# Order of the q, k and v weight loads between layers of a six-layer attention network

## What is computed

```python
def attn_layer(x, Wqkv, qs, ksc, Wo):
    qkv = x @ Wqkv                               # 128 x 3072 weights: q, k, v of 16 heads of 64
    q, k, v = jnp.split(qkv, 3, -1)
    ...
    q = l2norm(q) * qs
    k = l2norm(k) * ksc
    ...                                          # rotary tables on q and k
    out = local_attention(q, k, v)               # windows of 32 tokens, each sees itself and the one before
    return out @ Wo
for i in range(DEPTH):
    x = attn_layer(shift_tokens(x), Wqkv[i], ...) + x
    x = ffn_layer(shift_tokens(x), ln_g[i], ...) + x
```

## Time and profile before

| | |
|---|---|
| median of 3 runs | 2058.47 us (2055.76 to 2065.01) |
| the profiled execution, its own time | 2059.67 us |
| its span, first to last instruction | 2057.6 us |
| PE busy | 1890.4 us, 92% of the span |
| DVE, ACT, POOL busy | 66%, 58%, 58% |
| the network, first k projection of tile 0 to that of tile 95 | about 142 to 1799 us |
| mean granted clock of TensorE | 0.958 of full speed |

### The profile page before, as it was taken

How to read it: one execution, slowest core, us unless ns; L and a number is a source line. 1 busy time by engine, 2 the same in 40 slices (tenths; PEclk the granted TensorE clock), 3 DMA queues, 4 the chain that set the end, 5 groups by cost and what they waited for, 6 DMA issues and landing times. The chain is left out here.

```text
span 2057.6 us, 71282 instructions
## 1 busy us (share of the span) xinstructions
PE 1890.4 (92%) x30632; PEld 1191.6 (58%) x30632; DVE 1348.7 (66%) x1564; ACT 1188.7 (58%) x2030; POOL 1201.5 (58%) x1291
## 2 busy tenths in 40 slices
PE   5867999899999899998999998999989999986898
PEld 5734666565666466665656664666656566653444
DVE  5646777677777577776677775777766777742533
ACT  4425666466766666664667656666746676553333
POOL 0118777667776677776677766777766777630000
PEclk9979999999999999999999999999999999997888
DMA  1023222222222322223222222222232222201000
GB/s 46 0 86 74 69 63 64 82 62 73 72 61 64 79 70 73 62 64 82 64 72 72 62 63 78 71 72 61 66 83 62 73 72 62 64 20 46 6 5 11
DMA packets 84770, 125.11 MB, mean 61 GB/s; under 512 B 26208, under 2 KB 31976, under 8 KB 84336
## 3 DMA queue, kind: packets, MB, share of 16 engines
q1 hardware_dynamic: 84464, 120.64, 23.2%
HBM read 21.98 MB, written 1.05 MB: 11 GB/s over the span
## 5 line engine op out<-in xcount | busy, mean ns | idle before, releaser
L318 POOL TENSOR_TENSOR qkn<-t 128x1024 f32<-128x1024 f32 x192 | 452.5, 2357 | 258.7 <-DVE t L715 251.5
L309 POOL TENSOR_TENSOR qkn<-qkn,rn 128x512 f32<-128x512 f32 x384 | 392.5, 1052 | 14.6 <-POOL rn L303 1.3
L711 DVE TENSOR_TENSOR t<-qk_ps,rot 128x1024 f32<-128x1024 f32 x192 | 229.1, 1193 | 110.7 <-ACT sq L585 109.6
L326 POOL TENSOR_TENSOR pn<-pexp,rden 128x512 f32<-128x512 f32 x192 | 196.2, 1043 | 171.6 <-DVE rden L699 171.6
L585 ACT ACTIVATE sq<-qk_ps 128x1024 f32<-128x1024 f32 x192 | 196.7, 1025 | 147.9 <-PE qk_ps L383 125.2
L447 PEld LDWEIGHTS sc_ps<-prT,v_win 64*64 64x64 f32 x12288 | 199.8, 136 | 126.0 <-issue 125.8
L725 DVE TENSOR_REDUCE sums<-sq 128x16 f32<-128x1024 f32 x192 | 233.1, 1214 | 43.2 <-ACT sq L585 37.5
L578 ACT COPY prT<-ring 128x512 f32<-128x512 f32 x192 | 112.2, 584 | 243.2 <-PE ring L431 243.2
L398 PE MATMUL ring<-ident,qkn 128*128 128x128 f32 x1536 | 228.0, 282 | 23.2 <-POOL qkn L309 18.7
L715 DVE TENSOR_TENSOR t<-qk_ps,rot 128x1024 f32<-128x1024 f32 x192 | 232.9, 1213 | 0.0
L447 PE MATMUL sc_ps<-prT,v_win 64*64 64x32 f32 x12288 | 221.2, 221 | 7.8 <-DVE pr L687 6.4
(11 more groups left out here) (238 smaller groups left out, 2836.6 us busy)
## 6 DMA issues: line engine op xcount, KB each, us to landing
v_win<-v_tok SPq DMA_DIRECT2D x1488, 64.0 KB, 2.0
wqkv<-in_w_qkv SPq DMA_DIRECT2D x18, 512.0 KB, 4.1
wo<-in_w_o SPq DMA_DIRECT2D x6, 512.0 KB, 3.9
w<-in_w SPq DMA_DIRECT2D x6, 341.0 KB, 3.3
w<-in_w SPq DMA_DIRECT2D x6, 192.0 KB, 3.0
r_xtok<-in_x SPq DMA_DIRECT2D x4, 256.0 KB, 3.5
amask<-in_att_mask SPq DMA_DIRECT2D x1, 1024.0 KB
out_x<-xo SPq DMA_DIRECT2D x4, 256.0 KB, 2.3
```

The source lines that it names most:

```text
L309: nc.gpsimd.tensor_tensor(by_head(quarter(qkn, f)), by_head(quarter(qkn, f)), rn[:, 8 * f:8 * (f + 1)].unsqueeze(2).to_broadcast([P, 8, DH ...
L318: nc.gpsimd.tensor_tensor(half(qkn, k), half(t1, k), half(t2, k), ALU.add).then_inc((q_added, k_added)[k], 1)
L711: nc.vector.tensor_tensor(by_head(half(t1, k)), by_head(of), rot[:, l % 2, 2 * k, s:s + 1, :].to_broadcast([P, HEADS, DH]), ALU.mult).then ...
```

## The change

For the last tile of a layer SP now waits for k_full and loads k, waits for v_full and loads v, then does the waits and the 14 v moves as before, and after them waits for q_full and loads q. The loads of layer 0 are as they were, and nothing is changed on the other engines.

```diff
                     r, t = g // TILES, g % TILES
                     l, b = r // B, r % B
-                    if t == TILES - 1 and b == B - 1 and l + 1 < DEPTH:
-
-                        sp.wait_ge(q_full, 2 * (g + 1))
-                        load_qkv(l + 1, 0, s_wq)
+                    last_of_layer = t == TILES - 1 and b == B - 1 and l + 1 < DEPTH
+                    if last_of_layer:
+
                         sp.wait_ge(k_full, 2 * (g + 1))
                         load_qkv(l + 1, 1, s_wk)
+                        sp.wait_ge(v_full, 2 * (g + 1))
+                        load_qkv(l + 1, 2, s_wv)
                     sp.wait_ge(v_copied, 2 * (g + 1))
                     if g > 2:
 
                         sp.wait_ge(av_full, g - 2)
...
-                    if t == TILES - 1 and b == B - 1 and l + 1 < DEPTH:
-                        load_qkv(l + 1, 2, s_wv)
+                    if last_of_layer:
+                        sp.wait_ge(q_full, 2 * (g + 1))
+                        load_qkv(l + 1, 0, s_wq)
                     if l > 0 and b == 0 and t == TILES - 1:
```

## The result

The changed kernel takes 2005.3 us (median of 4 runs, 2001.07 to 2007.18) against 2059.75 us before (median of 4, 2055.76 to 2065.01): ratio 0.9731, 95% interval 0.9704 to 0.9759. Two further sets of five runs gave medians of 2002.9 and 2001.6, against 2058.0 and 2057.9 before. The profiled execution of the changed kernel, one of the four, took 2007.18 us with a span of 2005.3 us; that this span equals the median is chance.

A forecast was written before the change was run, and what follows sets the result against it. PE, busy 92%, sets the pace and idles for weights at changes of layer. Terms 11.7 + 31.8 + 9.5 - 2.5 give 50.5 us; the yardstick's 52.2 was taken, giving 2006.3 us against the median, range 2000 to 2018.

The forecast's parts named there:

- the sum: Whole kernel: the forecast's reckoning, 50.5 us by its terms and 52.2 us by the yardstick, of which 52.2 was taken.
- Steps 1 and 2: Changes of layer: k load issued first, v load next; PE's waits for k (11.7 us) and v (31.8 us) go.
- The yardstick: Five stage pairs at changes of layer, 218.6 us together, should take 33.28 us each as inside a layer: 52.2 us gained.
- Step 3: v matmuls at each change of layer: without a pause ahead they take the fast time, 1.9 us less each, 9.5 us.
- rival A: v matmuls at changes of layer stay slow because of freshly landed weights, not the pause: 9.5 us kept, 2015.8 us; chance 0.05.
- Step 4: v moves of a layer's last tile no longer wait for q_full: they start 4 us earlier and cost nothing.
- Step 5: q load after the moves: issued at 399.1, lands at 402.9, due at 405.8, 2.9 us to spare; the tightest place.
- rival B: q load at changes of layer lands 1.6 us late, 8 us in five: 2014.3 us; chance 0.08.
- Step 6: Transposes after each change of layer wait for POOL again, 0.5 us each: 2.5 us come back.
- Rival C: POOL becomes the bound behind the changes of layer: 20.5 us come back, 2026.8 us; chance 0.03.
- The terms: Listed effects at changes of layer: k wait 11.7, v wait 31.8, slow matmuls 9.5, less POOL 2.5: 50.5 us.
- Rival E: Slower: q held back on SP; gain of 10.4 us per change used up at landing 416.2; 2069 if 12.6 late; chance 0.02.

## Why the prediction was right

The forecast was 2006.3 us and the measured time 2005.3. The mechanism is the forecast's; that the two times meet within 1 us is in part luck. The gain by the medians of the three sets was 54.5, 55.1 and 56.3 us, 2 to 4 us above the 52.2 of the sum. The 95% intervals of the ratios include 52.2, and no run shows where more would come from. Point by point:

- **Steps 1 and 2** (the waits of k and v go) held: both rows are gone. That it was the weights that ended both waits is shown by the runs in which one of the two loads comes early and the other not, with v's wait rising to 43.3 us when k alone is early, and k's staying at 11.9 us when v alone is early. Their two terms are not independent, which the prediction did not say: k's 11.7 us are worth nothing unless v comes early too. The yardstick, which measures both together, does not depend on this.
- **Step 3** (the slow v matmuls go) held, and its reason too: with a pause alone, in front of weights that had landed long before, the group takes 3.75 us at a granted clock of 0.50. The prediction's point against rival A, that a k group behind a landing and a pause of 2.08 us stays fast, was weaker than it looked: with v alone early, k groups behind waits of 1.98 and 2.24 us were slow. It is the run with the pause alone that decides.
- **Step 4** (the v moves start 4 us earlier and cost nothing) held. The run that puts q ahead of them, and starts them 4 us later again, takes the same time.
- **Step 5** (q 2.9 us before its due time) held at the first change: q was issued 17.1 us after the last tile's k projection began, against 17.0 by the sum, and landed in 3.8 us. It was never waited for, but at the fourth change the issue came 1.4 us later than computed and the landing took 5.1 us, which left 0.3 us. So rival B came nearer than its chance of 0.08 suggests, and that no wait appeared there owes something to luck. Rival B had taken the price of lateness as 1 us for each us; the runs with q held back show that slow matmuls come on top, 0.3 to 3.2 us at a change.
- **Step 6** (2.5 us of waits for POOL come back) held. In the five pairs the transposes did not wait for POOL before, and now wait 0.51 to 0.58 us in each, 2.8 us in all. The wait over the network is a poorer measure: it was 21.2, 20.3 and 19.5 us in three profiles of the changed kernel, so that 21.2 less 18.7 is just the 2.5 forecast is chance. Rival C did not appear.
- **The sum.** The yardstick, the same pair of stages inside a layer, gave 52.2 us; the pairs became 51.9 us shorter. The terms gave 50.5, and the 1.4 us between lie in small gaps and slow matmuls that were not listed, such as the k group of 2.52 us at the second change, shown below.
- **Rival E** was far off in time, but its price was too low: with the 2.5 us of slow matmuls that a wait brought in the mean in the first run with q held back, the gain of 10.4 us at a change would be used up when q is about 8 us late, not 10.4. That is an estimate; the longest wait for q tried was 4.8 us.

Step 5 had cited a rule of the Trainium skill's page "DMA: Bandwidth & Descriptors", section "Queues, rings and completion order", that a load's completion waits for the writes ahead of it on the same engines. No run here shows it by itself. Five loads with no moves right ahead or behind took 3.3 to 4.4 us, median 3.4, and the five of the changed kernel behind 14 moves 3.7 to 5.1, median 3.8, so that the moves ahead account for about 0.4 us, if for anything. What did lengthen a landing was work issued behind it, on which I had not counted.

## What to carry to other kernels

When one buffer is refilled in parts, issue the loads in the order in which their readers come, and keep long runs of small DMAs out from between them; the exact moment of issue matters far less, as the run with the old issue time and the new order shows, where two loads of fifteen were 1 to 2 us late. Read the worth of such a change from the same stage where no refill happens, not from the sum of the waits: two waits in a row can be one delay, and the slow matmuls behind a pause belong to it.

## What the runs showed of the hardware that I had not expected

A late load costs more than its wait: 19.1 us of waits brought 12.5 us of slow matmuls with them. How long the wait lasts did not settle whether or how far the slow stretch follows. In front of q, 2.62 us did it, 2.72 us did not. In front of k, 1.98 and 2.24 us did it with v alone early, and 1.55 us did not. What decides it stays open. In the kernel before, 2.08 us in front of k left its four matmuls at 1.98 us, while 3.09 us at the second change of layer made them slower in part; the group and its stretch there:

```profile
682.55 2.52 PE L383 MATMUL qk_ps<-wqkv,state 128*128 128x512 f32 x4 [3.09 <-DMA wqkv<-in_w_qkv]
```

```profile
682.55:685.00 2.45, 2.45 (x4) 0.77 0.39 95
```

DMAs issued right behind a 512 KB load went with a longer landing, 4.6 against 3.6 us in the mean of five each.

The part of the program behind the network, which no run changed, took 252.8 to 260.1 us in the profiled executions. The stretch of PE in the two kernels compared, and in the run with q ahead of the moves:

```profile
1797.60:2057.60 260.00, 212.33 (x1477) 0.83 0.06 18
```

```profile
1746.90:2005.30 258.40, 210.62 (x1470) 0.83 0.06 19
```

```profile
1746.82:1999.60 252.78, 205.72 (x1473) 0.84 0.07 19
```

That is 7 us between executions of the same code, and most of what single executions differ by; PE's busy time differs by as much, at a granted clock of 0.83 to 0.84. It is why differences of 2 us could not be settled by the times here and had to be read from stages.
